# Inner rows of a tile's eight dense expert jobs, formed turned or turned afterwards

## The reference, cut to what matters

```python
for e in range(E):                                   # E = 8
    h = jax.nn.gelu(jnp.einsum('bsd,dh->bsh', xn, W1[e]) + b1[e], approximate=False)   # 256 -> 512
    y_e = jnp.einsum('bsh,hd->bsd', h, W2[e]) + b2[e]                                   # 512 -> 256
    y = y + y_e * w_full[..., e, None]               # w_full is 0 unless e is in the node's top two
```

## Time and profile before

| | us |
|---|---|
| median of 3 runs | 2450.99 |
| lowest, highest | 2449.42, 2451.27 |
| the profiled execution | 2453.85 |
| its span | 2452.1 |
| TensorE matmul busy | 1907.1 (78%) |
| VectorE busy | 1636.0 (67%) |
| ScalarE busy | 935.2 (38%) |
| GpSimd busy | 1684.2 (69%) |

### The profile page before, as it was taken

One profiled execution on the slowest core, in us unless ns is written; L12 is line 12 of the kernel. 1 busy time (PEld: TensorE's weight loads), 2 busy tenths in 40 slices (PEclk: granted clock), 3 DMA queues, 4 the chain that ended last, 5 costly groups with the idle time before them and its releaser, 6 DMA issues. The chain is left out here.

```text
span 2452.1 us, 36512 instructions
## 1 busy us (share of the span) xinstructions
PE 1907.1 (78%) x9170; PEld 1451.7 (59%) x9171; DVE 1636.0 (67%) x3697; ACT 935.2 (38%) x1485; POOL 1684.2 (69%) x1824
## 2 busy tenths in 40 slices
PE   4739999787787877667888878888777777887782
PEld 3627777566665655556666666666555555665551
DVE  4748888668788775877676667666565655765542
ACT  3523333336455543444343444443332323333230
POOL 0077777777777777777777777777777777777621
PEclk9869999888787878778999998999988888899896
DMA  7476665866666666666776777777777777777551
GB/s 229 165 152 174 169 164 151 285 189 184 178 180 175 179 177 172 172 168 185 193 201 192 202 200 205 206 197 196 202 204 201 202 196 199 201 205 197 162 154 49
DMA packets 298847, 454.53 MB, mean 185 GB/s; under 512 B 83487, under 2 KB 197648, under 8 KB 298110
## 3 DMA queue, kind: packets, MB, share of 16 engines
q0 software_dynamic: 85248, 237.14, 37.3%
q1 hardware_dynamic: 204092, 203.60, 28.3%
q10 hardware_dynamic: 9282, 11.22, 1.4%
HBM read 393.82 MB, written 62.13 MB: 186 GB/s over the span
## 5 line engine op out<-in xcount | busy, mean ns | idle before, releaser
L1230 POOL DMA_INDIRECT rows_g<-node_table,src_all x1568 | 1489.8, 950 | 478.4 <-issue 467.2
L1781 PE MATMUL psB<-rows_g,pick_e 128*128 128x260 f32 x3136 | 930.8, 462 | 321.7 <-issue 260.6
L1781 PEld LDWEIGHTS psB<-rows_g,pick_e 128*128 128x128 f32 x3136 | 718.1, 235 | 492.8 <-issue 352.8
L1652 ACT ACTIVATE pick_n<-local_row 128x1024 bf16<-128x1024 bf16 x196 | 207.1, 1057 | 796.3 <-PE psA L1770 750.0
L1312 DVE TENSOR_TENSOR rows_g<-rows_g,psD 128x2048 f32<-128x2048 f32 x196 | 446.3, 2277 | 0.0
L1301 DVE TENSOR_TENSOR p_both_e<-rows_g,psD 128x64 f32<-128x64 f32 x196 | 43.4, 222 | 350.3 <-DMA rows_g<-node_table,src_all 342.6
L1287 DVE TENSOR_TENSOR pick_e<-psD,slot_all 128x1024 f32<-128x1024 f32 x196 | 236.6, 1207 | 0.0
L1648 ACT ACTIVATE local_row<-local_row,minus_id 128x1024 bf16<-128x1024 bf16 x196 | 222.5, 1135 | 28.8 <-DMA local_row<-local_dram 22.1
L1816 PE MATMUL psC<-W_f,xnT 128*128 x468 | 220.6, 594 | 5.0 <-DVE hid L1344 5.0
L1853 PEld LDWEIGHTS psD<-W_f,hidT 128*128 128x128 f32 x936 | 177.9, 190 | 74.1 <-issue 56.0
L1853 PE MATMUL psD<-W_f,hidT 128*128 x936 | 221.1, 379 | 0.0
(11 more groups left out here) (288 smaller groups left out, 2297.6 us busy)
## 6 DMA issues: line engine op xcount, KB each, us to landing
local_row<-local_dram SPq DMA_DIRECT2D x196, 256.0 KB, 3.8
acc<-in_L_ffn_b_dram SPq DMA_DIRECT2D x125, 256.0 KB, 3.9
rows_g<-node_table,src_all POOLq DMA_INDIRECT x1568
acc<-in_L_ffn_b_dram SPq DMA_DIRECT2D x125, 128.0 KB, 4.5
xin<-sent_dram SPq DMA_DIRECT2D x117, 128.0 KB, 3.3
set_dram<-xn SPq DMA_DIRECT2D x117, 128.0 KB
xnT<-xnT_dram SPq DMA_DIRECT2D x96, 128.0 KB
node_table<-acc SPq DMA_DIRECT2D x7, 924.0 KB
```

Source lines behind the costliest of these rows:

```text
L1230: pool.indirect_dma_start(out=rows_g[:, r, j], out_offset=None, in_=node_table, in_offset=bass.IndirectOffsetOnAxis(ap=src_all[:, g, j:j + ...
L1652: act.activation(pick_n[:], local_row[:, r], ACT.Relu, bias=1.0, scale=-1.0).then_inc(pick_n_ready, 1)
L1781: last = pe.matmul(ps_sum[s % 2][:, 0:AW], pick_e[:, s % SLOTS, j], rows_g[:, s % RING, j, 0:AW], start=(j == 0), stop=(j == EG - 1))
```

## The change

For dense jobs the operands of up are exchanged: a 128 x 128 piece of the expert's `W1_f` is the stationary operand and the turned tile `xdT` (128 x 128) the moving one. The result has the hidden units in the partitions and the nodes in the free dimension, which is the form that `down` takes. It needs no turning. The bias is then one number per partition, and ScalarE's activation adds it; VectorE's addition, `turn_h` and `take_h` are gone for these jobs. Banks and buffers alternate by the job's parity: `ps_up` and `hidT` for even, `ps_hT` and `hid` for odd. All eight experts' biases come as columns in one load, issued by SP in step 92 into `hidden_cols`, 128 x 8 x 4. The 256 KB broadcast of the first bias goes for these jobs, the second bias is waited for in `result`.

```diff
+            hidden_cols = cells(5800, NE * HK).rearrange("p (e c) -> p e c", c=HK)
+            n_dense = min(n for n in job_step if job_at[job_step[n]][1] == "dense")
...
+            def hidden_of(a):
+                return hidT if a % 2 == 0 else hid[:].rearrange("p (c n) -> p c n", c=HK)
+            def hidden_bank(a):
+                return (ps_up, ps_hT)[a % 2]
...
+                    def hidden_columns():
+                        sp.dma_start(hidden_cols, fb1.rearrange("e (c p) -> p e c", p=P), allow_slow_non_contiguous=True).then_inc(cols_in, 16)
...
                     def bias_rows(n, e):
                         v = n % 4
                         sp.wait_ge(ys_ready, n - 3)
-                        sp.dma_start(bias_row[:, v, 0:H], fb1[e].partition_broadcast(P)).then_inc(bias_in[v], 16)
                         sp.dma_start(bias_row[:, v, H:], fb2[e].partition_broadcast(P)).then_inc(bias_in[v], 16)
...
+                            if job and job[0] == NT + 8:
+                                hidden_columns()
...
                         if kind == "dense":
                             dve.wait_ge(w_ready, 1)
+                            dve.wait_ge(bias_in[n % 4], 32 * bias_count[n] - 16 * (a // 4 + 1))
...
-                            if jobs_with(s - 1):
+                            if jobs_with(s - 1) and jobs_with(s - 1)[1] != "dense":
                                 hidden_bias(*jobs_with(s - 1))
...
+                    def dense_gelu(n, a):
+                        act.wait_ge(up_done, n + 1)
+                        act.wait_ge(cols_in, 16)
+                        if a == 0:
+                            act.wait_ge(down_done, n_dense)
+                        if a == 1:
+                            act.wait_ge(h_turned, n_dense)
+                        if a >= 2:
+                            act.wait_ge(down_done, n - 1)
+                        for c in range(HK):
+                            last = act.activation(hidden_of(a)[:, c], hidden_bank(a)[:, c * P:(c + 1) * P], ACT.Gelu, bias=hidden_cols[:, a, c:c + 1])
+                        last.then_inc(gelu_done, 1)
...
-                            if jobs_with(s - 2):
+                            if jobs_with(s - 2) and jobs_with(s - 2)[1] != "dense":
                                 take_h(*jobs_with(s - 2))
...
-                        if n >= 1:
+                        if n >= 1 and kind != "dense":
                             pe.wait_ge(hb_ready, n)
...
                             pe.wait_ge(xT_taken, turn_number[("tile", 0)] + 1)
-                            for c in range(KT):
-                                last = pe.matmul(ps_up[:, :], xdT[:, c], W1_f[:, a, c], start=(c == 0), stop=(c == KT - 1))
+                            if a == 0:
+                                pe.wait_ge(hb_ready, n_dense)
+                            if a == 1:
+                                pe.wait_ge(hT_ready, n_dense)
+                            if a >= 2:
+                                pe.wait_ge(gelu_done, n - 1)
+                            for c in range(HK):
+                                for k in range(KT):
+                                    last = pe.matmul(hidden_bank(a)[:, c * P:(c + 1) * P], W1_f[:, a, k, c * P:(c + 1) * P], xdT[:, k],
+                                                     start=(k == 0), stop=(k == KT - 1))
...
-                            if jobs_with(s - 2):
+                            if jobs_with(s - 2) and jobs_with(s - 2)[1] != "dense":
                                 turn_h(*jobs_with(s - 2))
```

More of the change, by code:

```diff
@@ L1024, in gps_layer @@
             rows_in, x1_in, y_out = ([sem(f"{n}{u}") for u in range(2)] for n in ("rows_in", "x1_in", "y_out"))
-            zero_out, relocated = sem("zero_out"), sem("relocated")
+            zero_out, relocated, cols_in = sem("zero_out"), sem("relocated"), sem("hidden_cols_in")
             y_ready, y0_ready, y0_out = sem("y_ready"), sem("y0_ready"), sem("y0_out")
@@ L1658, in take_x @@
                         act.activation(xnT[:, u], ps_xT[:, 0:KT * P].rearrange("p (k n) -> p k n", k=KT), ACT.Copy).then_inc(xT_taken, 1)
+                    def dense_gelu(n, a):
[10 more added lines that the diff above has]
+                        last.then_inc(gelu_done, 1)
                     def gelu(n, kind, a, k):
                         rows, cols = (tile_rows(a), D) if kind == "mix" else (P, H)
+                        if kind == "dense":
+                            dense_gelu(n, a)
+                            return
                         act.wait_ge(hb_ready, n + 1)
@@ L1843, in down @@
                     def down(n, kind, a, k):
-                        pe.wait_ge(hT_ready, n + 1)
+                        if kind == "dense":
+                            pe.wait_ge(gelu_done, n + 1)
+                        else:
+                            pe.wait_ge(hT_ready, n + 1)
                         if kind == "mix":
@@ L1855, in down @@
                             for c in range(HK):
-                                last = pe.matmul(ps_small[:, down_at], hidT[:, c], W2_f[:, a, c], start=(c == 0), stop=(c == HK - 1))
+                                last = pe.matmul(ps_small[:, down_at], hidden_of(a)[:, c], W2_f[:, a, c], start=(c == 0), stop=(c == HK - 1))
                         last.then_inc(down_done, 1)
```

## The result

The changed kernel takes 2438.61 us (median of 5 runs, 2437.44 to 2441.12), the kernel before 2450.99 (5 runs, 2449.01 to 2451.27): ratio 0.9951, 95% interval 0.9937 to 0.9964, so 12.4 us less (8.8 to 15.4). The profiled execution after takes 2439.75 us for a span of 2437.9, 14.2 us less span than before.

What follows compares the result with a forecast made beforehand. GpSimd's gathers were taken to pace the edge loop, and after it a TensorE-VectorE loop of 4.99 us per dense job. Steps of 3.52 us would bring the last combine 8.3 us earlier: 2450.99 - 8.3 = 2442.7 us, range 2439.8 to 2449.8.

Steps and rivals of the forecast that it cites:

- c6: Last of VectorE's seven combines of tiles 7 to 1 near the end; forecast at 2407.9 us, before 2416.21.
- the dense term: From the dense jobs to the last combine: a gain of 8.3 us, taken off the median.
- The new up: First product of a dense job on TensorE: 16 instructions at 0.112 us, 1.79 us, or 2.04 after a wait.
- rival A: Dense ups on TensorE: weight loads not hidden behind the stream, 0.22 us per instruction, 5.5 us slower, 2456.5; chance 0.08.
- Steps 0 to 6: TensorE's dense loop, numbered by the job whose up each holds; 3.52 us each from step 3, ending at 2388.97.
- step 1's wait for the copy: Second dense up waits for ScalarE's copy of the last block's rows: 0.60 us plus 0.15 for hand-overs.
- step 2's for gelu: Third dense up waits once for job 0's gelu on ScalarE: 1.26 us, 1.4 with hand-overs.
- The alternating chains: At the end, combines free buffers for GpSimd's collections; two such chains alternate, the even one ends last, rounds of 6.0 us.
- c0: First of VectorE's seven combines of tiles 7 to 1; forecast at 2389.87 us, before 2396.61.
- c2: Third of VectorE's seven combines of tiles 7 to 1; forecast at 2395.9 us, before 2404.12.
- The column load: Load of hidden_cols on SP's queue in the edge loop, 4,096 four-byte pieces: priced at nothing, 11.4 us without cover.
- rival D: At the end, both chains' collections meet on GpSimd and the queues, giving part of the gain back: 2445.7 us; chance 0.09.

Runs made afterwards that it cites:

- experiment 1: Changed kernel with satisfied waits added so every engine's code behind the dense jobs lies, modulo 256 instructions, as in the kernel before; ratio 0.9979.
- experiment 2: Kernel before with satisfied waits added so every engine's code behind the dense jobs lies, modulo 256 instructions, as in the changed kernel; ratio 0.9973.
- experiment 8: Changed kernel with satisfied waits (136 instructions) on TensorE alone, so only its code lies as in the kernel before; ratio 0.9968.
- experiment 10: Changed kernel with swapped hidden buffers, own banks for dense ups and earlier last combines, plus 80 instructions of satisfied waits on VectorE; ratio 0.9894.
- experiment 11: Changed kernel with only 80 instructions of satisfied waits added on VectorE in the edge loop; ratio 0.9949.
- Experiment 7: Changed kernel with the last set's seven combines, their rows' collection and their stores three steps earlier in the queues' order; ratio 0.9916.
- Experiment 3: Changed kernel with the column load of the first layer's bias issued four times in a row, three into unread cells; ratio 0.995.
- experiment 6: Changed kernel with the dense jobs' hidden buffers swapped and their ups in the two PSUM banks of the edge loop's sums; ratio 0.9931.

## Why the prediction was wrong, and where it was right

**The step that failed** is the last sentence on what bounds the kernel: "What follows to the end of the span (35.9 us) does not touch the change." The change does not touch that stretch's work, but it moves that stretch's code, and the stretch consists of branches over code. Experiments 1, 2 and 8 show it from both sides: the changed kernel with the old placement has the 35.9 us again, the kernel before with the new placement has 31.0, and 4.3 of the 5.6 us go with TensorE's placement alone. The part of the sum that was missing is a term of -5.6 us, put at nothing without a reason. The profiles bear the rest out: between the first dense up and c6 8.0 us against 8.3 forecast, behind c6 5.6 against 0, and 0.6 ahead of the first dense up that the forecast does not have, 14.2 in all. The timed runs are less kind to the 8.3: of the 12.4 us, 6.8 are left without the 5.6, and experiment 1 gives 5.2 (3.2 to 7.4). With both terms the median would have been forecast at 2437.1, and 2438.61 was measured. So the dense term may be too large by 1.5 to 3 us in the median, which hid part of the missing one; why is open. No rival could have led to the missing term, since each was a mechanism inside the dense jobs, their end or the edge loop.

What is not shown is the mechanism beneath. The counts that follow are of the compiled instructions. TensorE's fifth branch jumps over 318 instructions, counted with the labels in the listing. It starts at place 255 of a count modulo 256 before, where it is dear, and at 118 or 119 after, where it is cheap; the third (87 instructions) starts at 207 and at 70 or 71. The third, where dear, comes 1.5 to 1.8 us after the landing of another far jump. From 2415 us on, only queues of kind "instruction" move data in the changed kernel (packets, MB, share):

```profile
q8 instruction: 6, 0.10, 1.2%
q14 instruction: 16, 0.13, 1.1%
```

The Trainium skill ("Runtime: NRT & Kernel Launch", Instruction fetch mechanics) says that instructions are fetched in blocks of 16 KiB, 256 of them, and that a taken branch whose target lies outside the current window of two blocks has to wait for a fetch. TensorE's fifth branch agrees with it: with the block's border where the count puts it, the dear one passes two borders and the cheap one passes one. The third passes one border where it is dear and none where it is cheap, so the rule alone does not say why it waited; that the block behind the border was not yet there, so soon after the other jump, is a guess that no run tests. VectorE's fourth branch (333 instructions) does not: by the same count it passes one border in every placement tried (starting at 6, 15 and 86) and took 2.8 to 3.8 us in each. I tried it because a shifted border would have explained it, and experiments 10 and 11 said no. The rule for VectorE stays open.

**The new up**: 1.79 forecast, 1.78 measured; 2.04 behind a wait, 2.02 measured. The row of the narrow products was the right one, and rival A is out: 0.111 us per instruction with its load. The rule of the Trainium skill ("TensorE: Matmul & The Clock Gate", The mechanism) that I weighed there, that loads overlap only where the row groups differ, does not hold in this trace: load and stream together take 0.111 us, where 128 columns stream in 0.108 by the down's 0.216 for 256.

**Steps 0 to 6**: step 1's wait for the copy, step 2's for gelu, and 3.51 us a step from step 3 on are all in the chain; step 6's down ends at 2388.3, forecast 2388.97, of which 0.58 is the earlier start. Gelu was priced at 1.26 and took 1.14; it is on the path once.

**The alternating chains**: c0, c2 and c6 within 0.7 us. But my account of them took VectorE's order as given. Experiment 7 shows that this order was worth 8.3 us, as much as the change brought in the dense part.

**The column load, the bias rows and rival D**: nothing each, as priced. Experiment 3 shows the first. Rival D's late round did not occur in the changed kernel's profile; in those of experiments 6 and 8 one collection came late and c6 with it, by 1.6 to 2.3 us.

## What to carry to other kernels

A stretch in which no engine computes is not constant: where it consists of branches over code, as here, its length can depend on the count of instructions ahead of it. Here TensorE's code alone, moved by 136 instructions, made 4.3 us of difference. Before a small gain is credited to an idea, run the old kernel with the new kernel's instruction counts. And where a faster loop pays only through the order of a queue behind it, move what stands in that queue as well: three small edits to order and buffers brought more than the change itself.

## What the hardware showed that I had not expected

- A taken branch of TensorE costs 0.29 or 1.6 to 2.0 us, and another 0.41 to 0.49 or 3.7 to 4.1, over the same code, by its place.
- A load of 4,096 pieces of 4 bytes lands in 7.9 us in the edge loop, where loads of 128 KB (`xin`) land in 3.4, and the earlier trace rows would give 11.4. So it is not the size (16 KB) that sets its time, and the pieces are cheaper than the 48-byte ones of the earlier trace rows, which is a transfer of another stage. Four such loads in a row hold SyncE's queue for 16.5 us.
- An up that starts after a wait is 0.24 us longer than one that follows a product (2.02 against 1.78), about what the up of four instructions had over the down of equal columns (1.98 against 1.73).
